# Attention scores as two one-pass products of rounded parts and rests

## The reference

```python
h = concatenate([tok(x), txt], axis=1)                 # 32 x 274 x 192
h = h + attention(layernorm(h))                        # 12 heads of 16, causal
h = h + experts(layernorm(h))                          # 4 + 4 experts, capacity and drops
# attention:
q = rope(X @ Wq + bq);  k = rope(X @ Wk + bk);  v = X @ Wv + bv
scores = einsum('bqhd,bkhd->bhqk', qh, kh) / sqrt(16)
scores = where(causal, scores, -inf)
out = einsum('bhqk,bkhd->bqhd', softmax(scores), vh) @ Wo + bo
```

## Time and profile before

| | |
|---|---|
| time, three runs | 1395.81, 1400.01, 1387.93 us; median 1395.81 |
| span of the profiled execution, first to last instruction | 1318.5 us |
| busy: TensorE, VectorE, GpSimd, ScalarE | 1196.7, 887.9, 622.7, 555.8 us |
| granted TensorE clock, mean | 0.969 |
| maxima on TensorE (L564), scores (L591) | 1536 and 2304 instructions |
| transfers of mT (L462, L463) | 192 of 2 KB and 32 of 0.8 KB |

### The profile page before, as it was taken

The page is one execution under the profiler, slowest core; times in us unless marked ns, Lnnn a source line. Parts: engine busy times, 40 slices in busy tenths (PEclk is TensorE's granted clock), DMA queues, the critical chain, the costliest instruction groups (busy, mean ns, idle before and its releaser), DMA issues. The chain is left out here.

```text
span 1318.5 us, 33201 instructions
## 1 busy us (share of the span) xinstructions
PE 1196.7 (91%) x12722; PEld 1019.6 (77%) x12722; DVE 887.9 (67%) x1991; ACT 555.8 (42%) x959; POOL 622.7 (47%) x990
## 2 busy tenths in 40 slices
PE   5899999999999999999999999883899999999993
PEld 4667777777777777777777777663899899999993
DVE  5667677767777678678767777746897755545441
ACT  1234434444444433443443444441544455555550
POOL 4133333333543453444444454443452477775565
PEclk8899999999999999999999999995999999999997
DMA  6001121113321331232223221237887678987651
GB/s 212 28 23 42 43 70 49 42 47 93 105 62 58 106 100 61 81 119 68 81 77 103 80 80 37 92 95 249 287 279 253 191 253 262 308 259 267 219 185 35
DMA packets 84367, 168.03 MB, mean 127 GB/s; under 512 B 16446, under 2 KB 57701, under 8 KB 84208
## 3 DMA queue, kind: packets, MB, share of 16 engines
q1 hardware_dynamic: 70544, 139.88, 33.5%
q0 software_dynamic: 13664, 26.00, 5.5%
HBM read 123.83 MB, written 45.45 MB: 128 GB/s over the span
## 5 line engine op out<-in xcount | busy, mean ns | idle before, releaser
L759 ACT ACTIVATE PT<-round_banks 128x1752 f32<-128x1752 f32 x96 | 156.6, 1632 | 173.0 <-PE round_banks L591 173.0
L876 POOL TENSOR_SCALAR_AFFINE_SELECT PT<-PT 128x512 f32<-128x512 f32 x192 | 118.1, 640 | 208.9 <-ACT PT L759 208.4
L1765 ACT ACTIVATE Gl<-h_ps,W 128x256 f32<-128x256 f32 x264 | 115.5, 474 | 172.0 <-PE h_ps L1675 164.0
L1686 PE MATMUL y_ps<-W,Gl 128*128 128x192 f32 x1056 | 181.2, 325 | 0.0
L1686 PEld LDWEIGHTS y_ps<-W,Gl 128*128 128x128 f32 x1056 | 171.3, 189 | 0.0
L1675 PE MATMUL h_ps<-XH,Wh 128*128 128x256 f32 x528 | 147.5, 297 | 10.0 <-DVE Wl L1834 6.9
L511 PE MATMUL gen<-w_emb,xT 128*128 128x192 f32 (+1 forms) x768 | 141.8, 336 | 7.4 <-DMA ident<-in_ident_dram 7.4
L1675 PE MATMUL h_ps<-XH,Wl 128*128 128x256 f32 x528 | 140.1, 286 | 0.0
L994 DVE TENSOR_TENSOR capped<-round_banks,masks_f 128x1024 f32<-128x1024 f32 x96 | 116.3, 1211 | 32.7 <-PE round_banks L564 32.2
L511 PEld LDWEIGHTS gen<-w_emb,xT 128*128 128x128 f32 (+1 forms) x768 | 118.1, 170 | 15.6 <-DMA ident<-in_ident_dram 7.4
L591 PEld LDWEIGHTS round_banks<-QKT 32*128 32x128 f32 x2304 | 94.5, 186 | 42.6 <-DVE nm L996 23.0
(11 more groups left out here) (273 smaller groups left out, 2445.5 us busy)
## 6 DMA issues: line engine op xcount, KB each, us to landing
W<-in_experts_dram SPq DMA_DIRECT2D x44, 771.0 KB, 5.1
W<-in_experts_dram SPq DMA_DIRECT2D x44, 672.0 KB
xT<-in_xT_dram SPq DMA_DIRECT2D x32, 591.0 KB, 4.3
X<-sorted_d SPq DMA_DIRECT2D x35, 386.0 KB, 5.6
stage<-rows_d SPq DMA_DIRECT2D x64, 192.0 KB
rows_d<-h SPq DMA_DIRECT2D x32, 192.0 KB
out_dram<-h SPq DMA_DIRECT2D x32, 192.0 KB
rows_d<-xn SPq DMA_DIRECT2D x32, 192.0 KB
```

The lines of the kernel that those rows point to most:

```text
L759: act.activation(PT[(JG * b + j) % 2][:], R[:, :, 0:438], ACT.Exp, scale=SCALE).then_inc(exps, 1)
L876: pool.affine_select(x[:, :, at:at + P], x[:, :, at:at + P], [[0, GH], [1, P]], ALU.is_ge, 0.0, base=0, channel_multiplier=-1)
L1686: mm = pe.matmul(y_ps[t.par][:, k * D:(k + 1) * D], Gl[t.par][:, f, k * P:(k + 1) * P], W[t.i][:, W2O + f * D:W2O + (f + 1) * D], start=(f ...
L1765: act.activation(Gl[t.par][:, f, :], h_ps[f % 3][:, 0:ROWS], ACT.Gelu, bias=W[t.i][:, B1O + f:B1O + f + 1]).then_inc(g_ready, 1)
```

## The change

Queries and keys are kept as a rounded part (fp32r, which TensorE multiplies in one pass) and a rest, in `HX` (128 x 2 x 6 x 322; index 0 the rounded part "hi", index 1 "lo"). `rr` now holds each head twice in its 32-row slot, and VectorE forms in `lo` the rest in rows 0 to 15 by `low * hi + g` and the whole value in rows 16 to 31. One product over 32 rows and one over 16 (or 18) rows give the score. Row 16 and 17 of a slot carry the maximum's two parts, so `mT` has two halves and is sent twice. The tail maxima stay f32, with their queries in `Qt`. V and Vt slots shrink from 32 to 17 columns. The bank of a head slot is emptied by VectorE in place of ScalarE. `values(fin, 1)` moves ahead of the first maxima. Fills at the start change with it (QKT, rr and rrt are no longer cleared, R's last part is), and the input `slots` (128 x 3) is new.

```diff
-        QKT = [sb(f"QKT{i}", [P, 2 * JG, 3 * P]) for i in range(3)]
-        V = [sb(f"V{i}", [P, 2, HEADS, SLOT]) for i in range(4)]
+        HX = [sb(f"HX{i}", [P, 2, 2 * JG, KW], F32R) for i in range(3)]
+        V = [sb(f"V{i}", [P, 2, HEADS, HD + 1]) for i in range(4)]
-        mT = sb("mT", [P, P])
+        mT = sb("mT", [P, 2, P], F32R)
...
@@ SP, for image t.mid
-                    for j in range(JG):
-                        for k in range(2):
-                            sp.dma_start(q[HD:P:SLOT, j, tok(k)], mT[12 * j + 2 * k:12 * j + 12:3, :]).then_inc(mrow_in[b % 2], 16)
-                    sp.dma_start(q[HD:P:SLOT, 0:JG, 2 * P:S], mT[36:40, ...]).then_inc(mrow_in[b % 2], 16)
+                    for w in range(2):
+                        q, m = HX[b % 3][HD + w:P:SLOT, 1].bitcast(F32), mT[:, w, :].bitcast(F32)
+                        for j in range(JG):
+                            for k in range(2):
+                                sp.dma_start(q[:, j, tok(k)], m[12 * j + 2 * k:12 * j + 12:3, :]).then_inc(mrow_in[b % 2], 16)
+                        sp.dma_start(q[:, 0:JG, 2 * P:S], m[36:40, ...]).then_inc(mrow_in[b % 2], 16)
@@ TensorE, maxs
                 for k, at in ((1, P), (0, 0)):
-                    for i in range(GH):
-                        rows = slice(SLOT * i, SLOT * (i + 1))
-                        mm = pe.matmul(R[:, i, at:at + (k + 1) * P], q[rows, j, tok(k)], q[rows, JG + j, 0:(k + 1) * P], start=True, stop=True, ...)
+                    keys = slice(0, (k + 1) * P)
+                    for q, x, n, first in ((hi, lo, SLOT, True), (lo, hi, HD, False)):
+                        for i in range(GH):
+                            rows = slice(SLOT * i, SLOT * i + n)
+                            mm = pe.matmul(R[:, i, at:at + (k + 1) * P], q[rows, j, tok(k)], x[rows, JG + j, keys], start=first, stop=not first, ...)
@@ TensorE, scores
-                    pe.wait_ge(mrow_in[b % 2], 112 * (b // 2 + 1))
+                    pe.wait_ge(mrow_in[b % 2], 224 * (b // 2 + 1))
                 for klo, qlo, n, at in ((0, 0, S, 0), (P, P, S - P, S), (2 * P - o, 2 * P, TL, 2 * S - P)):
-                    (four f32 products, one a head, of 32 rows, 128 keys)
+                    m = min(P, KW - klo)
+                    for x, q, deep, first in ((lo, hi, SLOT, True), (hi, lo, HD + 2, False)):
+                        for i in range(GH):
+                            rows = slice(SLOT * i, SLOT * i + deep)
+                            mm = pe.matmul(R[0:m, i, at:at + n], x[rows, JG + j, klo:klo + m], q[rows, j, qlo:qlo + n], start=first, stop=not first, ...)
@@ TensorE, order in a turn
+                if t.fin is not None:
+                    values(t.fin, 1)
                 if t.mid is not None:
                     (wait for KQ0 to KQ2)
                     maxs(t.mid, 0)
                 if t.fin is not None:
-                    values(t.fin, 1)
                     values(t.fin, 2)
@@ ScalarE, copy_heads; the tails likewise, in four copies in place of two
-                emptied(f"KQ{c}", b, act.activation(QKT[b % 3][:, 2 * c:2 * c + 2, 0:2 * P], ..., ACT.Copy))
+                for lo, hi in ((0, 1), (1, 2)) if c == 1 else ((0, 2),):
+                    dst, src = HX[b % 3][:, 0, 2 * c + lo:2 * c + hi, 0:2 * P], g[:, lo:hi, :]
+                    if 2 * c + lo < JG:
+                        ins = act.activation(dst, src, ACT.Copy)
+                    else:
+                        ins = act.activation(dst, src, ACT.Identity, scale=keep, bias=unit)
+                ins.then_inc(heads_rounded, 1)
@@ ScalarE, MT
-                    emptied("MT", t.mid, act.activation(mT[:], g[:, 0:P], ACT.Copy))
+                    act.activation(mT[:, 0, :], g[:, 0:P], ACT.Copy).then_inc(m_rounded, 1)
@@ GpSimd, rope_add (for the tails likewise)
+                pool.wait_ge(rr_added, 2 * b + k + 1)
+                pool.tensor_copy(rr[:, k, :, HD:SLOT], rr[:, k, :, 0:HD]).then_inc(rr_ready, 1)
@@ VectorE, new
+            def rest(dst, hi, g):
+                return dve.scalar_tensor_tensor(dst, hi.bitcast(F32), low, g, ALU.mult, ALU.add)
+            def rest_heads(b, c):
+                g = take(f"KQ{c}", b)[:].rearrange("p (j t) -> p j t", j=2)
+                dve.wait_ge(heads_rounded, JG * b + c + 1)
+                js = slice(2 * c, 2 * c + 2)
+                emptied(f"KQ{c}", b, rest(HX[b % 3][:, 1, js, 0:2 * P], HX[b % 3][:, 0, js, 0:2 * P], g))
+            def rest_tails(g):  (two such, of 288 and 144 columns)
@@ VectorE, order in a turn
                     rotate("QK1", ...)
+                if t.tail[1] is not None:
+                    rest_tails(t.tail[1])
                     (reduce_max(t.mid, 2), the tail maxima, L1209, choose, position)
+                if t.pre is not None:
+                    rest_heads(t.pre, 0)
+                    rest_heads(t.pre, 1)
+                if t.mid is not None:
+                    g = take("MT", t.mid)
+                    dve.wait_ge(m_rounded, t.mid + 1)
+                    emptied("MT", t.mid, dve.tensor_tensor(mT[:, 1, :], g[:, 0:P], mT[:, 0, :].bitcast(F32), ALU.subtract))
                     (rotation of the tails, their norm and scaling)
+                if t.pre is not None:
+                    rest_heads(t.pre, 2)

```

More of the change, by code:

```diff
@@ L21 @@
 JG, GH, SLOT = 3, 4, 32
+KW = 322
 IMG1 = 1 + NPATCH - P
@@ L287, in attention @@
         att = sb("att", [P, 2, D])
+        biasb = att
         attT = sb("attT", [KC + 1, 2, 2 * P])
@@ L2002, in build @@
     return nc
-IN_NAMES = ["xT", "txt", "ident", "masks", "tmask", "cosw", "sinw", "base", "biasb", "w_emb", "w_qkv", "w_o", "w_r", "rconsts", "before", "experts"]
+IN_NAMES = ["xT", "txt", "ident", "masks", "tmask", "slots", "cosw", "sinw", "base", "biasb", "w_emb", "w_qkv", "w_o", "w_r", "rconsts", "before", "experts"]
 def layout(I):
@@ L2019, in layout @@
     o["tmask"] = np.where(i[None, :TL] > i[:, None] % SLOT, BIG, 0.0).astype(np.float32)
+    row = i[:, None] % SLOT
+    first, sums = row < HD, (row >= HD) & (row < HD + 2)
+    o["slots"] = np.concatenate([np.where(first, -1.0, 0.0), np.where(sums, 0.0, 1.0), np.where(sums, 1.0, 0.0)], 1).astype(np.float32)
     inv = (1.0 / np.float32(10000.0) ** (np.arange(D // 2, dtype=np.float32) * np.float32(2.0) / np.float32(D))).astype(np.float32)
```

82 lines of the change are left out of this document (46 added, 36 removed).

## The result

The changed kernel takes **1545.5 us** (median of four runs, 1544.4 to 1548.9) against 1395.8: a ratio of 1.117, 95% interval 1.112 to 1.123. On another chip, experiment 9, it took 1536.2 (1528.3 to 1545.3) against 1393.8, a ratio of 1.101 (1.094 to 1.109). The forecast of 1495 us had the direction and the mechanism; its range ended at 1531 and did not hold the time. Runs over 1.5% above the fastest of their kernel are left out of the ratios; the profiles of experiments 3 and 13 are of such runs.

The account below looks back on a forecast made before the run. TensorE's own list sets the pace now; afterwards the chain through fourteen serial transfers takes over. Chain +73 us and lowered clock +26 us make +99 on 1395.8: 1495 us, range 1455 to 1531.

Parts of the forecast that it names:

- The chain that takes over: Fourteen serial issues on SP's queue, score block, embedding and VectorE's work set the turn: 2.29 us a turn more, +73 us.
- Rival 2: On SP's queue, the second seven transfers cost no issue time: some +15, 1410 us; chance 0.08.
- rival 3: In the attention stage, the chain stays under TensorE's path and 39 us are gained: 1357 us; chance 0.06.
- TensorE's blocks: Score blocks 0.21 us and maxima 0.20 us shorter on TensorE, narrow groups gaining nothing: 1.23 us a turn.
- Rival 4: On TensorE, one-pass groups run one after another or narrow ones no faster: 1505 us or beyond 1600; chance 0.05.
- The range's lower bound: 1455 us: the chain decides, the clock holds (1469 us), and narrow groups on TensorE take half the time.
- VectorE's additions: Three products with sum (0.6 us each), a subtraction and tail products on VectorE: 2.2 us a turn beside a 73% load.
- The clock: TensorE idles 2.8 us before the first score block, then runs at 1.2 GHz in two turns of three: +26 us.
- The sum: Attention-stage terms of +99 us added to the whole kernel's 1395.8, giving 1495 us.
- the upper bound, 1531: Whole time with the clock's upper bound, 1523 us, and 8 us for 0.25 us a turn in the extras.

Follow-up runs that it names:

- experiment 9: The changed kernel again, with no edit, on another chip: 1536.2 us against 1393.8, ratio 1.101.
- experiments 3: Changed kernel with only the first seven transfers, the low part of the row of maxima left out: 1418.1 us, ratio 1.019.
- 13: Changed kernel with six extra instructions, half of the embedding's first product again, ahead of the first score block: 1528.1 us, ratio 1.092.
- Experiments 2: Kernel before with seven more transfers per image into an unread buffer, first score block waiting for all fourteen: 1443.2 us against 1391.3, ratio 1.039.
- 6: Changed kernel with the first seven transfers started without waiting for VectorE's subtraction, still fourteen issues: 1474.8 us, ratio 1.068.
- 7: Changed kernel with six wider transfers in place of fourteen, and nine small matmuls in place of one transpose: 1456.1 us, ratio 1.056.
- 14: Changed kernel with fourteen transfers and one transpose, first seven sent early, VectorE's order changed: 1470.6 and 1476.5 us, ratio about 1.055.
- both fillers: Changed kernel with the embedding's first product repeated ahead of the first score block, wholly (1524.1 us) or half (1528.1 us).
- experiment 12: Changed kernel with six packed transfers, first ones early, VectorE reordered, first score block behind the embedding's second half: 1571.8 us, ratio 1.129.

## Why the prediction was right or wrong

- **The chain that takes over: right**, and to a few hundredths of a microsecond. Last minimum to first issue 3.75 for 3.73 forecast (2.9 and the 0.825 a turn for choice and positions), issues 7.79 for 7.75, addition to last minimum 12.72 for 12.71. The 3.73 are in part luck: in the turn with the positions the prediction's own rows give 2.27 + 1.6 = 3.9 us, where it wrote 2.9 + 1.5, and the trace has 4.56, with 0.58 in it in which VectorE waits for ScalarE's copy. Experiments 2 and 3 change the number of issues, 6 their start, 7 number and start, and the time follows each. Rival 2 (the second seven for nothing) and rival 3 are refuted by 2 alone. The Trainium skill (DMA: Bandwidth & Descriptors, Anatomy of one DMA) says of transfers on GpSimd's path that completion and not set-up makes up most of the fixed cost. These transfers, on SyncE's queue, don't follow that: 0.54 us of issue each, one after another, against one landing of 1.07.
- **TensorE's blocks: right, a little low.** At full clock a score block now takes 0.81 us (504.30 to 505.11) and a block of maxima 0.61 (520.03 to 520.64), where 0.84 and 0.67 were forecast: narrow groups gain some 0.03 each, far from half. Rival 4 is refuted. (The range's lower bound was 7 us too low for its reason: narrow groups at half save another 0.21 us on the chain, which gives 1469 - 7 = 1462 and not 1455.) By the fast weight load of the Trainium skill (TensorE: Matmul & The Clock Gate, Weight-path perf modes) the prediction would have had some 6 us less, 0.2 us on the score block; the trace shows 0.03.
- **VectorE's additions: their length was low, their place on the chain right.** A rest takes 0.75 us, not 0.6. The two ahead of the first issue lie beside ScalarE's copies, so that the path grew by no more than forecast. The subtraction (0.28) and GpSimd's copy (0.50) were as assumed, ScalarE's copies a little over it (0.54 a turn more, 2.33 against 1.79). That the third rest would be covered as much as it adds was only right for three turns in four: in the fourth it stands behind the tail's scaling, and TensorE waits up to 4.0 us for it.
- **The clock: too small a term.** The prediction put it at 1.2 us in two turns of three, 0.81 a turn, behind the first score block alone. There it was 4.33 - 3.40 = 0.93 a turn (1.37 in the second profile), though the stretch came out at 4.33 for the 4.28 forecast, as at full clock it is 3.40 and not 3.47. In 11 of 26 turns the addition came 1.5 to 2.9 us late. Set beside the wait ahead of the score block, in six profiles (after twice, 2, 6, 13 and 14; a fall is a stretch to the addition of over 4.6 us where 3.3 to 3.7 is the rule, and the clock records have a stretch at 0.50 in each of them and in no other):

| TensorE's wait | cases | clock fell behind it |
|---|---|---|
| 0.15 to 1.8 us | 51 | 1 |
| 1.8 to 2.3 us | 31 | 18 |
| 2.5 to 3.3 us | 25 | 22 |

It also came where it wasn't looked for. In one turn TensorE ran at 0.50 from 591 to 604 us, through the end of the turn, with a wait of 1.37 us for the tail's rotation in its midst, and came to the score block 3.85 us after the last issue, 2.8 us later than the landing would have let it:

```profile
580.00:590.50 10.50, 9.38 (x132) 6.66 (x130) 10.31 (x19) 4.09 (x7) 5.06 (x9) 1.00 0.16 55
591.00:604.00 13.00, 11.63 (x56) 9.79 (x57) 5.51 (x16) 5.29 (x10) 3.15 (x7) 0.50 0.01 3
604.50:612.00 7.50, 7.50 (x116) 6.39 (x116) 5.43 (x13) 2.90 (x4) 2.02 (x5) 1.00 0.59 184
```

This turn and one more (image 22, with a wait of 2.09 us for the same rotation) make up 0.28 us of the 0.33 by which the stretch before the score block is longer than forecast. What fell at 591 isn't clear from the rows: the waits in the 10 us before it are 0.91 us and shorter. The price was taken from a stretch of 3.4 us; this one has 13. Over the attention stage the clock stood at 0.50 for 188 us, against 14 before.
- **The sum: wrong in what it left out.** Per turn 30.00 - 29.55 = 0.45 us from the above and 0.13 because before's mean turn is 26.32 and not the 26.46 of the four turns in the earlier trace rows: 19 us over 32 turns. Another 10 us come at both ends of the stage, where turns of 27.8 and 34.1 us stand for 22.1 and 22.7. Then 3 to 7 us at the start and 16 to 29 in the experts' stage (6 to 15 by the medians), which the prediction took as nothing. With the 99 that were forecast this makes 147 to 164; the spans differ by 153 and 163.

**The step that failed** is the one from the stage to the whole: the sum was made for the attention stage and compared with the whole time, with nothing for the start and the experts' stage. Attention alone, +128 and +134 us, lies inside the +135 that the upper bound, 1531, allows. With the 7 and 3 us of the start the two profiles stand at 1530 and 1532, at the bound itself; what took the time over it is the experts' stage. Inside the attention stage the terms that were too small are the clock, the middle turns of before and the ends of the stage, 29 us together in the first profile.

Still open: why the experts' stage differs by up to 46 us between kernels that give it the same code and work (and by 63 us between two profiles of the kernel before itself), and how much of the loss the low clock makes in all. What it puts on the chain was measured; that it is worth that much when removed was not, as both fillers gave it back ahead of the score block.

## What to carry to other kernels

Each of these small transfers within on-chip memory cost SyncE's queue 0.54 us to issue, with pieces of 512 bytes as with 1096. So count such transfers, not their bytes, and before doubling them find the slack: the same seven cost 52 us where 2.8 us a turn were free and some 125 where that was used up. A chain can be forecast well from one turn of the profile (29.55 us a turn against 30.00 and 30.33), but the whole time has other stages too, which need a term of their own in the sum and the range. Waits that a change adds to TensorE should be priced twice: by their length, and by what the clock loses behind them. Of the 56 waits of 1.8 to 3.3 us counted here, 40 had 1.3 to 2.9 us lost behind them. What a change brings as a side effect (here a block moved ahead of a wait) may be its only good part, so run it by itself.

## What the runs showed of the hardware

- Six transfers with pieces of 1096 bytes issue in 3.23 us, six with pieces of 512 in 3.24.
- The longer TensorE's wait, the more often the clock fell behind it, as the table above counts, but the low stretches have very different lengths: after 2.87 us 15 us of gapless work at 0.50 (experiment 12), after 2.70 us less than 5, and 13 us in a stretch with no wait over 0.91 us ahead of it.
- fp32r products with 16, 18 or 32 rows share the array by rows as f32 ones do: the 24 instructions of a score block (274, 146 and 18 columns, 3504 in all) take 0.81 us, 0.23 ns a column, where one that has the array to itself took 0.47. In f32 the block took 1.05.
- A product with sum of 128x512, one operand in PSUM and one in SBUF, takes VectorE 0.747 us, where its reduction of the same size from PSUM takes 0.681.
